# Mean layers of a graph network: gathered rows in 32 slots of 512 bytes, one semaphore for each of eight quads, and residual rows loaded in parts

## What is computed

```python
deg = jax.ops.segment_sum(jnp.ones(src.shape[0], x.dtype), dst, num_segments=n)
inv_deg = (1.0 / jnp.maximum(deg, 1.0))[:, None]

def sage_conv(h, Wl, b, Wr):
    agg = jax.ops.segment_sum(h[src], dst, num_segments=n) * inv_deg
    return agg @ Wl + b + h @ Wr
h = jax.nn.relu(sage_conv(x, W_l0, b0, W_r0))
h = jax.nn.relu(sage_conv(h, W_l1, b1, W_r1))
return sage_conv(h, W_l2, b2, W_r2)
...
x = _layernorm(x + _L2_gnn_ref(...), axis=-1)
```

## Time and profile before

| | |
|---|---|
| median of 3 runs | 9533.67 us (9487.52 to 9561.22) |
| span of the profiled execution | 7176.9 us |
| the three mean layers within that span | about 4700 to 5960 us |
| PE / DVE / POOL / ACT busy over the span | 77% / 66% / 69% / 31% |
| mean granted TensorE clock | 0.854 of full speed |

### The profile page before, as it was taken

One profiled execution on the slowest core, in us unless ns is written; L12 is line 12 of the kernel. 1 busy time (PEld: TensorE's weight loads), 2 busy tenths in 40 slices (PEclk: granted clock), 3 DMA queues, 4 the chain that ended last, 5 costly groups with the idle time before them and its releaser, 6 DMA issues. The chain is left out here.

```text
span 7176.9 us, 119509 instructions
## 1 busy us (share of the span) xinstructions
PE 5508.6 (77%) x30303; PEld 4146.7 (58%) x30345; DVE 4723.0 (66%) x20399; ACT 2257.9 (31%) x5949; POOL 4949.5 (69%) x5131
## 2 busy tenths in 40 slices
PE   5575667776777767777767777789899997888887
PEld 4442344555666555666656666666666665666665
DVE  7985667466666556666636666664545546888887
ACT  1044442211114411113411111543333333445444
POOL 5777765577777577777477777647576674777774
PEclk6687888778888878888878888899999998989888
DMA  9433352567777567777567777667576762222222
GB/s 305 138 80 86 81 112 51 155 201 210 208 208 220 166 188 209 208 207 218 178 175 210 208 208 209 198 182 211 164 211 188 211 207 75 56 56 57 56 56 53
DMA packets 911843, 1151.30 MB, mean 160 GB/s; under 512 B 143281, under 2 KB 676465, under 8 KB 911249
## 3 DMA queue, kind: packets, MB, share of 16 engines
q1 hardware_dynamic: 689440, 673.54, 31.0%
q0 software_dynamic: 202464, 461.07, 24.0%
q10 hardware_dynamic: 19346, 9.66, 0.5%
HBM read 882.09 MB, written 261.74 MB: 159 GB/s over the span
## 5 line engine op out<-in xcount | busy, mean ns | idle before, releaser
L500 POOL DMA_INDIRECT G<-table_kv,idx x2496 | 2386.9, 956 | 951.1 <-issue 748.3
L1718 DVE SCALAR_TENSOR_TENSOR sums<-ramp,place,bank 128x128 f32<-128x128 f32 x2496 | 717.6, 342 | 1160.4 <-PE bank L1635 1066.8
L1625 PE MATMUL bank<-ident,G 128*128 128x128 f32 x2496 | 642.3, 334 | 688.2 <-DMA G<-table_kv,idx 680.6
L2152 POOL DMA_INDIRECT G<-table_h,src_idx x864 | 831.1, 962 | 461.1 <-issue 252.4
L1604 ACT COPY slab<-bank 128x512 f32<-128x512 f32 x624 | 364.7, 584 | 2260.3 <-PE bank L1625 2259.7
L500 POOL DMA_INDIRECT G<-table_h,idx x832 | 833.4, 1002 | 302.0 <-issue 230.7
L1635 PE MATMUL bank<-qT,slab 128*128 x4992 | 910.2, 340 | 98.4 <-issue 78.6
L1635 PEld LDWEIGHTS bank<-qT,slab 128*128 128x128 f32 x4992 | 798.1, 243 | 195.0 <-issue 193.7
L1625 PEld LDWEIGHTS bank<-ident,G 128*128 128x128 f32 x2496 | 379.3, 163 | 904.5 <-DMA G<-table_kv,idx 862.8
L1849 DVE TENSOR_SCALAR OH<-ramp,place,weight 128x128 f32<-128x128 f32 x2136 | 737.0, 355 | 19.3 <-issue 10.6
L2136 PE MATMUL bank<-sums,qT 128*128 128x418 bf16 (+1 forms) x3528 | 676.5, 334 | 36.3 <-DVEq L2212 12.7
(11 more groups left out here) (355 smaller groups left out, 9482.1 us busy)
## 6 DMA issues: line engine op xcount, KB each, us to landing
stash<-G SPq DMA_DIRECT2D x312, 512.0 KB
sums<-stash SPq DMA_DIRECT2D x624, 256.0 KB
sums<-adjacency SPq DMA_DIRECT2D x294, 522.5 KB
adjacency<-same SPq DMA_DIRECT2D x49, 1184.0 KB
same<-adjacency SPq DMA_DIRECT2D x90, 522.5 KB
G<-table_kv,idx POOLq DMA_INDIRECT x2496
sums<-adjacency SPq DMA_DIRECT2D x48, 408.0 KB
table_kv<-G SPq DMA_DIRECT2D x72, 256.0 KB, 3.3
```

Of the source, the lines that this page charges most:

```text
L500: pool.indirect_dma_start(G[:, s, 0:width], None, tab, bass.IndirectOffsetOnAxis(ap=idx[:, s:s + 1], axis=0)).then_inc(c_gather[s].sem, 16)
L1625: ins = pe.transpose(bank[q % 2][:, (s % QUAD) * P:(s % QUAD + 1) * P], G[:, s, 0:D], ident[:])
L1718: ins = dve.scalar_tensor_tensor(scratch[:, s, :], ramp[:], place[:, n * QUAD + s:n * QUAD + s + 1], bank[2 + q % 2][:, s * P:(s + 1) * P] ...
L2152: pool.indirect_dma_start(G[:, s, 0:D], None, table[l], bass.IndirectOffsetOnAxis(ap=src_idx[:, DENSE + t:DENSE + t + 1], axis=0)).then_in ...
```

## The change

- `G` is seen as 32 slots of 512 bytes (`row_slots`), eight quads (`ROW_QUADS`). The memory is the same. `OH` keeps 16 slots.
- POOL waits from the 33rd gather on, for the quad that is eight back.
- The four gathers of a quad count on one semaphore, of eight in all. TensorE waits once for each quad, for 64, in place of four times for 16.
- The residual is loaded in four pieces in another order and to other places: blocks 0 to 15 to `slab`, the last block to `dst_part`, then blocks 16 to 31 and 32 to 47 to `slab`, each after the piece before it was added. They are added behind quads 12, 13, 28 and 44 in place of 12, 16, 17 and 34.
- The register load at line 921 is written in another form.

```diff
-                        _, (whole_at,) = nc.values_load_multi_w_load_instructions(
-                            chunk_wait[0:1, c:c + 1], engines=(SP,), min_val=1, max_val=TURNS_DENSE,
-                            skip_runtime_bounds_check_because="a number of turns, and 1 at least")
+                        whole_at = sp.value_load(chunk_wait[0:1, c:c + 1], min_val=1, max_val=TURNS_DENSE)
...
+        ROW_QUADS = 2 * QUADS
+        row_slots = G_flat.rearrange("p (s d) -> p s d", d=D)
...
-                s = t % SLOTS
-                if t % QUAD == 0 and t >= SLOTS:
-                    pool.wait_ge(c_rows.sem, c_rows.at(t // QUAD + 1 - QUADS))
-                pool.indirect_dma_start(G[:, s, 0:D], None, table[l],
-                                        bass.IndirectOffsetOnAxis(ap=src_idx[:, DENSE + t:DENSE + t + 1], axis=0)).then_inc(c_gather[s].sem, 16)
+                q = t // QUAD
+                if t % QUAD == 0 and q >= ROW_QUADS:
+                    pool.wait_ge(c_rows.sem, c_rows.at(q + 1 - ROW_QUADS))
+                pool.indirect_dma_start(row_slots[:, t % (ROW_QUADS * QUAD), :], None, table[l],
+                                        bass.IndirectOffsetOnAxis(ap=src_idx[:, DENSE + t:DENSE + t + 1], axis=0)).then_inc(c_gather[q % ROW_QUADS].sem, 16)
...
+            pe.wait_ge(c_gather[q % ROW_QUADS].sem, c_gather[q % ROW_QUADS].at(16 * QUAD * (q // ROW_QUADS + 1)))
             for k in range(QUAD):
-                s = q % QUADS * QUAD + k
-                pe.wait_ge(c_gather[s].sem, c_gather[s].at(16 * (q // QUADS + 1)))
-                ins = pe.matmul(bank[SUM_BANKS[q % 3]][:, k * P:(k + 1) * P], G[:, s, 0:D], OH[:, s, :], start=True, stop=True)
+                ins = pe.matmul(bank[SUM_BANKS[q % 3]][:, k * P:(k + 1) * P], row_slots[:, q % ROW_QUADS * QUAD + k, :], OH[:, q % QUADS * QUAD + k, :], start=True, stop=True)
...
-        RESIDUAL_QUADS = (EARLY_QUADS + 8, EARLY_QUADS + 12, EARLY_QUADS + 13, EARLY_QUADS + 30)
-        FIRST_RESIDUALS = 3
+        RESIDUAL_QUADS = (EARLY_QUADS + 8, EARLY_QUADS + 9, EARLY_QUADS + 24, EARLY_QUADS + 40)
+        FIRST_RESIDUALS = 2
+        RESIDUALS = len(RESIDUAL_QUADS)
...
-            b0 = (0, SLAB_BLOCKS, BLOCKS - 1, 2 * SLAB_BLOCKS)[r]
-            slab_rows = slab[:, 0:SLAB_BLOCKS * D].rearrange("p (b d) -> p b d", d=D)
-            home = (slab_rows, G[:, :, D:2 * D], dst_part[:, 0:D].unsqueeze(1), slab_rows)[r]
+            b0 = (0, BLOCKS - 1, SLAB_BLOCKS, 2 * SLAB_BLOCKS)[r]
+            home = dst_part[:, 0:D].unsqueeze(1) if r == 1 else slab[:, 0:SLAB_BLOCKS * D].rearrange("p (b d) -> p b d", d=D)
...
-                        sp_residual(FIRST_RESIDUALS)
-                    sp_adjacency(FIRST_STEPS + BLOCKS // 2, STEPS)
+                        sp_residual(2)
+                    sp_adjacency(FIRST_STEPS + BLOCKS // 2, FIRST_STEPS + BLOCKS)
+                    if l == 2:
+                        sp.wait_ge(residual_added.sem, residual_added.at(3))
+                        sp_residual(3)
+                    sp_adjacency(FIRST_STEPS + BLOCKS, STEPS)
```

More of the change, by code:

```diff
@@ L2279, in sums_passed @@
         def sums_passed():
-            for c in c_gather:
-                c.passed(16 * (RUN // SLOTS))
+            for k in range(ROW_QUADS):
+                c_gather[k].passed(16 * QUAD * len(range(k, RUN_QUADS, ROW_QUADS)))
             for k, c in enumerate(adj_in):
@@ L2437, in build_program @@
             if l == 2:
-                residual_in.passed(16 * (FIRST_RESIDUALS + 1))
-                residual_added.passed(FIRST_RESIDUALS + 1)
+                residual_in.passed(16 * RESIDUALS)
+                residual_added.passed(RESIDUALS)
         wup = wts[:, 0:D]
```

## The result

| | before | after |
|---|---|---|
| median | 9517.68 us (13 runs, 9486.54 to 9561.22) | 9569.81 us (13 runs, 9548.37 to 9590.32) |
| profiled execution, span | 7176.9 us (from another chip, as argued below) | 9579.5 us (device time 9581.34 us) |
| mean granted clock in it | 0.854 | 0.740 |

The ratio is 1.0054, with a 95% interval from 1.0040 to 1.0068. The change costs 52 us. I had forecast 9526.0 us with a range of 9470 to 9560, so the time lies outside the range, on the other side.

What follows compares the result with a forecast made beforehand. TensorE was taken to bound the mean layers; the only nonzero term was -7.7 us for its waits at the quads, all others 0, so 9533.67 - 7.7 = 9526.0 us, with a range of 9470 to 9560 us.

Steps and rivals of the forecast that it cites:

- The span and the median: The profiled span of 7176.9 us lay 2356.8 us below the runs' median; the saving was carried over unscaled.
- I take them for late rows: TensorE's 18 short "issue" waits at the mean layers' quads were gathered rows arriving late; the deeper ring would save 7.7 us.
- the waits don't go: Rival, chance 0.10: TensorE's short waits at the quads are not late rows, so nothing is gained, 9533.7 us.
- Earlier gathers: Sixteen more gathers a layer during TensorE's first steps cost 0; if fully exposed, 4.8 us a layer, +14.4 us in all.
- My rival on the other side: Chance 0.08: the additional gathers delay matrix loads of the first steps and TensorE waits; +6.7 us, 9540.4 us.
- The deeper ring's lead: With 32 slots POOL runs 20 us ahead of TensorE; its wait at a layer's start falls from 30.59 to about 10 us.
- The tail: At layer ends DVE sets the end, so removing TensorE's 7.1 us of waits on the gather's DMA gains 0.
- One wait in place of four: At each quad, 3 x 216 waits leave TensorE's queue; waits already satisfied cost nothing, so 0.
- the residual: In layer 2, the reordered residual loads and adds cost 0, up to +5 us if the cover fails.
- the loads: Ten added pairs of register-load instructions on SP, bounded by 5.6 us, stand ahead of waits and cost 0.
- The reverse side of the single wait: A quad's first matmul waits for all four gathers, up to 3.75 us later; covered by the 20 us lead.
- The range: 9470 to 9560 us, set by run scatter: from the near end of a POOL-bound rival to the highest run shown.

Runs made afterwards that it cites:

- e4: The full change against the kernel before, on a fast-kind chip where before took 7163.93 us: ratio 0.9996.
- j2: The full change with DVE's extra adds spread, against the kernel before, on a slow-kind chip where before took 9523.53 us: ratio 1.0051.
- j1: The kernel before with its old ring and waits, plus the new register load and spread extra adds, on a slow-kind chip: ratio 1.0003.
- e1: The kernel before with the new register load alone, on a fast-kind chip: ratio 1.0003 to the kernel before.
- e2: The kernel before with the new register load and new residual order, on a fast-kind chip: ratio 0.9995 to the kernel before.
- e3: The kernel before with new register load, new residual order and one wait a quad, still 16 slots, on a fast-kind chip: ratio 0.9996.
- j3: The full change against the kernel before, on a slow-kind chip where before took 9523.53 us: ratio 1.0056.
- i2: The full change against the kernel before, on a fast-kind chip where before took 7152.44 us: ratio 0.9999.

## Why the prediction was wrong

**The span and the median.** I found 2356.8 us between them and carried the saving over "as it is". This was the first failing step: the difference was no fixed cost but another kind of chip, so that no row that I had read described the runs that I forecast. The page of the profile after the change has 1.8 us between device time and span. The Trainium skill ("Runtime: NRT & Kernel Launch") puts the fixed cost of a launch near 15 us; no run here shows it, and neither figure explains the difference.

**"I take them for late rows": -7.7 us.** This step failed. The profile named no releaser, and I chose the supply because POOL showed a short wait at the same place. DVE's add came late and TensorE waited for the bank; POOL's wait for TensorE that I took for the partner came 7.6 us behind, so it can't have caused it. With the rows 20 us early the waits stayed at 7.5 us in 16 places; with 9 adds in place of 10 they went. My rival "the waits don't go", to which I gave 0.10, was what happened on the fast kind, and it also had the right reason against my reading, the missing releaser.

**"Earlier gathers": 0.** This is the term that decided the sign, and the step that failed on the chips that were timed. On the fast kind it holds (e4: busy 20 of 20 us). On the slow kind it is +20.8 us in the second layer's first steps, of which 5.5 us come back later, and much the same in the other two, 47 us in all. My rival on the other side had the right place, sign and trigger, but the wrong mechanism and price: it had TensorE wait for a late matrix load and the cost bounded by bandwidth, 4.8 us a layer. The measured cost is about the additional length of the burst, 16 x 1.25 = 20.0 us, since TensorE nearly stops while POOL issues them. The Trainium skill ("DMA: Bandwidth & Descriptors", on arbitration) says that each DMA engine serves its queues in turn. That is not what cost the time here: the DMA engines are busy for 0.29 of the burst, and no wait for a matrix load stands in it.

**The deeper ring's lead.** On the fast kind as foreseen: POOL's wait at a layer's start fell from 30.59 us to 6.2 to 6.9 (I had said 10), and in the second layer its last gather is issued 19 us ahead of TensorE's last quad (I had said 20). On the slow kind the wait is 40.67 us in j2 against 40.48 with the old ring in j1, since TensorE was late by as much as POOL was ahead.

**The tail: 0.** Right. The 7.1 us at the gather's DMA went, and TensorE's wait for the layer's end grew from 6.1 to 9.3 us in e4: the time moved from one wait into the other.

**One wait in place of four, the residual, the loads: 0 each.** Right on the fast kind, where e1, e2 and e3 lie within 0.05% of 1. The reverse side of the single wait that I had named, up to 3.75 us at a stalled quad, shows in e3, which has it with the old ring:

```profile
PE bank L2174 <- DMA G<-table_h,src_idx: 12.1, 3, 4.2
```

The three waits stand in front of the last quad of each layer, where DVE sets the end, and cost nothing that can be measured. On the slow kind the load is cleared by j1. The wait and the residual by themselves were not run there; the loss lies ahead of the first quad and as much in layers without residual, where neither acts.

**The range.** It reached from 9470 to 9560 us and rested on scatter within one kernel's runs. With a trace whose span was 25% off the runs, the far end of "earlier gathers", fully exposed, should have been priced in issue time (+60 us) and not in bandwidth (+14.4 us). Then 9560 would not have been the upper end.

## What to carry to other kernels

Where the profiled span and the timed median differ by far more than the scatter of the runs, the trace is from other conditions than the runs; widen the range before costing any edit from it. An unnamed short wait at an instruction that waits for several semaphores should be tried against each of them, the one that frees its output bank included, and sized by the weight loads' row beside the matmuls'. And a deeper ring of gathers by indirect DMA moves its producer's work into one unbroken burst at the start: what it costs the other engines there can exceed what the lead gives, as on the slow kind here, so look whether they slow down while that producer runs.

## What the runs showed of the hardware

- The same kernel takes about 7160 us on one kind of chip and about 9520 us on another, with nearly the same busy times of DVE, ACT and POOL (within 0.5%: 4738.7, 2246.6 and 4936.7 us in j3 against 4724.1, 2256.9 and 4943.4 in i2). I had not expected that one program's time could differ by a third between chips.
- On the slower kind TensorE and DVE issue single instructions in multiples of about 0.70 us while POOL issues indirect DMAs 1.25 us apart (1.28 for the scatters). It sets in 8 to 14 us after the first of them, and TensorE recovers 4 to 6 us after the last. The Trainium skill ("Runtime: NRT & Kernel Launch", the section on instruction fetch) says that an engine fetches its instructions ahead in blocks and that the cost of crossing a block is mostly hidden. The fast kind's traces agree (20 of 20 us busy beside gathers); if the crawl is that supply, which no run shows, the slow kind's do not, with 16 matmuls in the additional 22 us.
- The granted clock falls with it, to 0.61 in j2's burst against 0.96 behind it, so at the lower of its two levels (1.2 GHz) in much of it. It is not the cause: a matmul of 272 columns goes from 0.12 us to 0.23 us a piece, while the waits between them reach 2.4 us, and the first of them (7090.38) comes 2 us before the records lengthen.
